# Attention probabilities turned by VectorE block transposes and DMA instead of TensorE, and the rotation split over VectorE, ScalarE and GpSimd

## The chip, the cores and the metric

The kernel runs on one core of one Trainium2 chip. The metric is the device time of one execution in microseconds (us). Engines: TensorE (PE, with its weight loads PEld), VectorE (DVE), ScalarE (ACT), GpSimd (POOL) and SyncE (SP), which here only issues DMAs. SPq and ACTq are the queues of SyncE and ScalarE. A line such as L305 is a line of the kernel before; lines of the changed kernel are named as such.

## What is computed

For each of 32 batches of 256 tokens with 128 features (cut from the reference):

```python
xn = layernorm(x)
# attention on xn
h = layernorm(xn) * ln_scale + ln_bias
c_q, c_kv = h @ w_down_q.T, h @ w_down_kv.T              # 64 latents each
q, k, v = (c @ w_up.T for ...)                           # 16 heads of 64
q, k = rope(q), rope(k)                                  # neighbouring columns e, o:
#   e*cos - o*sin, e*sin + o*cos
attn = softmax(q @ k.T / 8)                              # 256 x 256 per head
a = (attn @ v, heads side by side) @ w_out.T + xn
# feed-forward on xn, then 5 steps of an integrate-and-fire count
y = square(relu(xn @ W_fc.T)) @ W_proj.T
out = x + a + count_of_spikes(y) / 5
```

## The kernel before, in words

The unit of work is a pair of heads (128 rows: two heads of 64). A batch has 8 pairs, the program 256, numbered g. Each engine runs the same list of 256 steps plus some ahead of them. In step g it treats pair g + LEAD of each stage, so that pair g's stages lie in different steps: project 5 ahead, rotation 4, rounding 4 and 3, scores 2, transposes 1, weighing 0. `p` = g modulo 8 is the place of the step in its batch; work that occurs once a batch (normalising inputs, latents, feed-forward, output) hangs on certain p. Two batches (16 steps) are one loop body. Engines wait for one another by counting semaphores only, and each engine takes its list in order.

The stages of one pair:

- **project** (PE, L281, L282): q and k of the pair, 128 rows by 256 tokens each, into the one bank ps_qk; four fp32r matmuls (weights as high and low part).
- **rotate** (DVE, L604): two instructions multiply ps_qk by cosine and sine into cos_sin. **exchange** (SP, L242): two DMAs of 128 KB swap neighbouring rows of the sine part (odd rows to even, even to odd) into sin_sw. **add_rotated** (POOL, L745): qk = cosine part + sin_sw.
- **leading** (ACT, L498) and **rest** (POOL, L751): qk is split into two fp32r parts, qk_hi and qk_lo.
- **scores** (PE, L295): twelve fp32r matmuls (low x high, high x low, high x high, for two token halves t and two heads h); the heads use rows 0 to 63 and 64 to 127. Results stand in two banks, ps_s0 and ps_s1, one buffer each.
- **row_max** (DVE, L613): one per head; **exponentials** (ACT, L490): four, with sums into den; result prob.
- **transpose_probs** (PE, L305): eight 128x128 transposes into ps_t; **copy_transposed** (ACT, L503): two copies to prob_t.
- **weigh_latents** (PE, L319): four fp32 matmuls against the latents ckv into ps_u (the trace has two instructions for an fp32 matmul, so eight); **copy_u** (ACT, L510).

Once a batch: two halves of the feed-forward (PE L353, L363; ACT relu; POOL square), the count (DVE L666, L669, `integrate`, from a copy `drive` of y in SBUF), reciprocals of the sums (DVE L620 to L626, `invert_sums`), `normalise_u` (DVE L634, four), `attention_out` (PE L395, four steps with four instructions each), `add_spikes` (DVE L677), `finish` (DVE L684), input loads and output stores (SP L231, L235), `moments_of` (DVE L640, L646), `split_latents` (DVE L653, L658).

What sets the order is the list of each engine, written by hand in its `step` with the leads of one table:

```python
LEAD = {"project": 5, "add": 4, "lead": 4, "rest": 3, "scores": 2, "transpose": 1, "multiply": 0}
```

PE takes scores, transposes, projection, the once-a-batch work of this p, weighing. DVE takes the two row_max, then once-a-batch work, rotate, and more of it. ACT takes the exponentials, copy_transposed, leading, once-a-batch work, copy_u.

## Time and profile before

| | |
|---|---|
| median of 3 runs | 1274.29 us (1272.05 to 1274.43) |
| the profiled execution's own time | 1276.49 us |
| its span | 1274.4 us |
| busy: PE, DVE, ACT, POOL | 95%, 75%, 84%, 63% |
| mean granted clock of TensorE | 0.993 |
| one batch in mid-run (8 steps) | 38.97 us |
| moved by DMA | 80.03 MB, mean 63 GB/s |

The profiled execution is 2.1 us longer than its span (work around the first and the last instruction). Busy time is a union over instructions of an engine; a row's mean duration can be longer than its busy time divided by its count, since consecutive instructions overlap. GB/s and DMA shares are over the core's 16 DMA engines.

### The profile page before, as it was taken

The page shows a single profiled execution, that of the slowest core. Times are in us where ns is not written, and L with a number is a line of the kernel's source. Part 1 is how long each engine was busy: PE and PEld are TensorE (multiplying, and loading weights), DVE is VectorE, ACT ScalarE, POOL GpSimd, SP SyncE. Part 2 cuts the span into 40 slices and gives each one's busy share as a digit, 9 for nine tenths or more (in the row PEclk, how much of TensorE's full clock was granted, in tenths as well). Part 3 has the DMA queues.
Part 4 walks back from the last instruction along what each step waited for, and adds up shares of the span by engine and source line. Part 5 has one row for each costly group of instructions (what it writes and reads, how often), then busy time and mean ns, then how long its engine had stood idle before and what let it go on. Part 6 is the DMA issues. An engine that isn't in the chain of part 4 may idle for free.

```text
span 1274.4 us, 33640 instructions
## 1 busy us (share of the span) xinstructions
PE 1209.4 (95%) x9952; PEld 942.4 (74%) x9952; DVE 954.2 (75%) x1734; ACT 1074.4 (84%) x3425; POOL 806.8 (63%) x773
## 2 busy tenths in 40 slices
PE   4899999999999999999999999999999999999997
PEld 3767777777777777777777777777777777777775
DVE  3677777877778777778777778777778777778774
ACT  1788888888888888898888888888988888988884
POOL 2766676656666666666656667566666666666561
PEclk9899999999999999999999999999999999999999
DMA  4111111111111111111111111111111111111110
GB/s 132 68 55 59 60 67 68 58 60 57 65 67 63 62 61 55 66 66 59 66 53 63 66 61 64 62 58 63 62 62 67 58 58 66 60 65 66 59 63 21
DMA packets 60065, 80.03 MB, mean 63 GB/s; under 512 B 9664, under 2 KB 26304, under 8 KB 59840
## 3 DMA queue, kind: packets, MB, share of 16 engines
q1 hardware_dynamic: 59968, 79.11, 17.4%
q14 instruction: 81, 0.66, 0.2%
q8 instruction: 16, 0.26, 0.1%
HBM read 7.77 MB, written 4.19 MB: 9 GB/s over the span
## 4 chain that ended last, share of the span: by engine, by line
PE 59%; issue 18%; DVE 9%; POOL 8%; ACT 4%; DMA 1%; DVEq 0%; ACTq 0%; POOLq 0%; SPq 0%
PE ps_t L305 12%; PE ps_u L319 12%; PE ps_s L295 12%; PE ps_b L395 6%; PE ps_a L363 3%; PE ps_a L353 3%; POOL qk_lo L751 3%; PE ps_qk L281 3%; ACT prob L490 3%; DVE cos_sin L604 3%; PE ps_qk L282 3%; POOL qk L745 2%; PE ps_b L387 2%; DVE latent L653 2%; DVE neg_max L613 2%
## 5 line engine op out<-in xcount | busy, mean ns | idle before, releaser
L490 ACT ACTIVATE prob<-ps_s,neg_max 128x256 f32<-128x256 f32 x1024 | 473.0, 477 | 106.3 <-DVE neg_max L613 80.3
L751 POOL TENSOR_TENSOR qk_lo<-qk,qk_hi 128x512 fp32r<-128x512 f32 x256 | 327.4, 1279 | 328.8 <-ACT qk_hi L498 328.7
L613 DVE TENSOR_REDUCE neg_max<-ps_s 128x2 f32<-128x512 f32 x512 | 329.8, 686 | 247.3 <-PE ps_s L295 246.4
L745 POOL TENSOR_TENSOR qk<-cos_sin,sin_sw 128x512 f32<-128x512 f32 x256 | 334.9, 1308 | 83.7 <-DMA sin_sw<-cos_sin 81.3
L604 DVE TENSOR_TENSOR cos_sin<-ps_qk,rope_sb 128x512 f32<-128x512 f32 x512 | 328.8, 683 | 18.0 <-PE ps_qk L282 15.6
L305 PE MATMUL ps_t<-ident_sb,prob 128*128 128x128 f32 x2048 | 279.7, 280 | 0.4 <-ACT prob_t L503 0.4
L503 ACT COPY prob_t<-ps_t 128x512 f32<-128x512 f32 x512 | 278.1, 610 | 0.0
L319 PE MATMUL ps_u<-prob_t,ckv 128*64 128x256 f32 x2048 | 277.6, 392 | 0.0
L305 PEld LDWEIGHTS ps_t<-ident_sb,prob 128*128 128x128 f32 x2048 | 222.1, 141 | 31.2 <-issue 1.0
L490 ACT ACTIVATION_READ_ACCUMULATOR prob<-ps_s,neg_max 128x1 f32 x1024 | 211.1, 206 | 0.0
L319 PEld LDWEIGHTS ps_u<-prob_t,ckv 128*64 128x64 f32 x2048 | 124.2, 136 | 97.9 <-issue 48.2
L295 PE MATMUL ps_s<-qk_hi,qk_lo 64*128 64x256 f32 x1024 | 172.1, 331 | 13.7 <-ACT prob L490 13.3
L498 ACT CAST qk_hi<-qk 128x512 fp32r<-128x512 f32 x256 | 168.5, 658 | 16.3 <-POOL qk L745 15.4
L295 PEld LDWEIGHTS ps_s<-qk_hi,qk_lo 64*128 64x128 f32 x1024 | 98.0, 185 | 113.3 <-issue 112.4
L281 PE MATMUL ps_qk<-latent,wup_hi 128*128 128x256 f32 x512 | 155.8, 326 | 3.5 <-DVE cos_sin L604 3.5
L295 PE MATMUL ps_s<-qk_lo,qk_hi 64*128 64x256 f32 x1024 | 146.0, 279 | 0.0
L295 PE MATMUL ps_s<-qk_hi 64*128 64x256 f32 x1024 | 145.6, 278 | 0.0
L395 PE MATMUL ps_b<-u_n,wvo_sb 128*128 128x256 f32 x512 | 132.8, 383 | 0.8 <-DVE u_n L634 0.8
L282 PE MATMUL ps_qk<-latent,wup_lo 128*128 128x256 f32 x512 | 132.8, 281 | 0.0
L510 ACT COPY u_raw<-ps_u 128x256 f32<-128x256 f32 x256 | 104.4, 408 | 3.5 <-PE ps_u L319 3.5
L395 PEld LDWEIGHTS ps_b<-u_n,wvo_sb 128*128 128x128 f32 x512 | 95.7, 192 | 12.9 <-DVE u_n L634 1.0
L281 PEld LDWEIGHTS ps_qk<-latent,wup_hi 128*128 128x128 f32 x512 | 97.9, 191 | 4.4 <-DVE cos_sin L604 4.0
(64 smaller groups left out, 1440.9 us busy)
## 6 DMA issues: line engine op xcount, KB each, us to landing
sin_sw<-cos_sin SPq DMA_DIRECT2D x512, 128.0 KB, 2.1
x_sb<-in_x SPq DMA_DIRECT2D x32, 128.0 KB, 2.1
out<-out_sb SPq DMA_DIRECT2D x32, 128.0 KB, 2.0
wup_raw<-in_wup SPq DMA_DIRECT2D x2, 512.0 KB, 5.6
rope_sb<-in_rope SPq DMA_DIRECT2D x1, 512.0 KB, 6.6
wo_sb<-in_wo_t SPq DMA_DIRECT2D x1, 512.0 KB, 7.8
sel_raw<-in_sel SPq DMA_DIRECT2D x1, 512.0 KB, 8.6
wfc_sb<-in_wfc_t SPq DMA_DIRECT2D x1, 256.0 KB, 6.7
```

Of the source, the lines that this page charges most:

```text
L281: nc.tensor.matmul(bank, wup_hi[:, which, cols], rhs, start=True, stop=False)
L282: last = nc.tensor.matmul(bank, wup_lo[:, which, cols], rhs, start=False, stop=True)
L295: mm = nc.tensor.matmul(ps_s[h][:, t, :], q[rows, par, 0, t * P:(t + 1) * P], k[rows, par, 1, :], start=(n == 0), stop=(n == len(parts) - 1))
L305: last = nc.tensor.transpose(ps_t[h][:, kt, t * P:(t + 1) * P], prob[:, s % 2, h, t, kt * P:(kt + 1) * P], ident_sb[:, :])
L319: last = nc.tensor.matmul(ps_u[h * L:(h + 1) * L, 0:S], ckv[:, (s // PAIRS) % 2, kt, :], prob_t[:, s % 2, h, kt, :], start=(kt == 0), stop ...
L395: last = nc.tensor.matmul(ps_b[:, 0:S], wvo_sb[:, pair, :], u_n[:, pair, :], start=(pair == 0), stop=(pair == PAIRS - 1))
L490: last = nc.scalar.activation(prob[:, s % 2, h, t, :], ps_s[h][:, t, :], ACT.Exp, bias=neg_max[:, s % 2, h, t:t + 1], accum_out=den[:, bpa ...
L503: nc.scalar.copy(prob_t[:, s % 2, h, :, :], ps_t[h][:, :, :]).then_inc(pt_ready[h], 1)
L604: last = nc.vector.tensor_tensor(cos_sin[:, s % 2, :, which, :], ps_qk[:, which, :].unsqueeze(1).to_broadcast([P, 2, S]), rope_sb[:, which ...
L613: nc.vector.tensor_reduce(neg_max[:, s % 2, h, :], ps_s[h][:, :, :], AXIS_X, ALU.max, negate=True).then_inc(max_ready[h], 1)
L745: nc.gpsimd.tensor_tensor(qk[:, s % 2, :, :], cos_sin[:, s % 2, 0, :, :], sin_sw[:, s % 2, :, :], ALU.add).then_inc(rope_done, 1)
L751: nc.gpsimd.tensor_tensor(qk_lo[:, s % 2, :, :], qk[:, s % 2, :, :], qk_hi[:, s % 2, :, :].bitcast(F32), ALU.subtract).then_inc(lo_ready, 1)
```

## The change

- The scores are computed from qk in plain fp32: four matmuls (eight instructions) in place of twelve; qk_hi, qk_lo, the ACT cast and the POOL subtraction are gone. ps_s has two buffers (four banks).
- The rotation: DVE multiplies ps_qk by the cosine into qk (one instruction); ACT copies ps_qk as it is to `raw`; for two pairs at once ACT issues the two row-exchange DMAs (256 KB each) from its own queue, raw to `partner`; POOL multiplies partner by the sine and adds it to qk.
- The probabilities: ACT writes them so that the four 32-column blocks lie apart; DVE transposes all 32x32 blocks of a pair in one instruction (`turn`, 1024 elements a partition) into `turned`; for each GROUP of four pairs SP issues 16 DMAs (`move`, 128 KB each, from 32 partitions to 32 partitions) to `gathered`, which the weighing matmuls read. The eight PE transposes and the two ACT copies are gone.
- DVE reads y for the count from PSUM (the copy `drive` is gone); row_max is one instruction for both heads.
- Leads: project 11, rope 9, scores 7, turn 6. The once-a-batch work moves to other p.

The diff, cut to its core:

```diff
-LEAD = {"project": 5, "add": 4, "lead": 4, "rest": 3, "scores": 2, "transpose": 1, "multiply": 0}
-FIRST = -6
+LEAD = {"project": 11, "rope": 9, "scores": 7, "turn": 6, "multiply": 0}
+FIRST = -LEAD["project"]
+GROUP = 4
+Q = P // 32
...
+        turned = sb("turned", [P, 2, Q, GROUP, S])
+        gathered = sb("gathered", [P, 2, Q, GROUP, 2, 2, TT, 32])
+        raw = sb("raw", [P, 2, 2, 2, S])
+        partner = sb("partner", [P, 2, 2, 2, S])
+        qk = sb("qk", [P, 4, 2, S])
+        ps_s = pb("ps_s", [P, 2, 2, TT, S])
...
+            def move(g, s, half):
+                par = (s // GROUP) % 2
+                if half == 0:
+                    sp.wait_ge(turn_done, done(g))
+                    sp.sem_inc(sp_waited, 1)
+                    sp.wait_ge(u_ready, done(g - 2 * GROUP))
+                for rows in (2 * half, 2 * half + 1):
+                    for block_of in range(Q):
+                        sp.dma_start(gathered[32 * block_of:32 * block_of + 32, par, rows, :, :, :, :, :],
+                                     turned[32 * rows:32 * rows + 32, par, block_of, :, :]).then_inc(moved[par], 16)
...
+                if (s + turn) % GROUP == GROUP - 1 and not outside(g + turn, STEPS):
+                    move(g + turn, s + turn, 0)
+                if (s + turn) % GROUP == 0 and not outside(g + turn - 1, STEPS):
+                    move(g + turn - 1, s + turn - 1, 1)
...
             def scores(g, s):
-                pe.wait_ge(lo_ready, done(g))
-                for h in range(2):
-                    pe.wait_ge(exp_done[h], done(g - 1))
+                pe.wait_ge(rope_done, done(g))
+                pe.wait_ge(exp_done, done(g - 2))
...
+                        last = nc.tensor.matmul(ps_s[:, s % 2, h, t, :], qk[rows, s % 4, 0, t * P:(t + 1) * P],
+                                                qk[rows, s % 4, 1, :], start=True, stop=True)
...
             def weigh_latents(g, s, i):
-                for h in range(2):
-                    pe.wait_ge(pt_ready[h], done(g))
+                if s % GROUP == 0:
+                    pe.wait_ge(moved[(s // GROUP) % 2], (i * (BODY // GROUP // 2) + s // GROUP // 2 + 1) * 16 * Q * Q)
...
+            def copy_projected(g, s, i):
+                duo = s // 2
+                act.wait_ge(cos_ready, done(g))
+                if s % 2 == 0 and not outside(g - 4, STEPS):
+                    act.wait_ge(swapped[duo % 2], (i * (BODY // 4) + duo // 2) * 32)
+                nc.scalar.copy(raw[:, duo % 2, s % 2, :, :], ps_qk[:, :, :]).then_inc(raw_ready, 1)
+
+            def exchange(g, s):
+                duo = s // 2
+                act.wait_ge(rope_done, done(g - 4))
+                act.sem_inc(act_waited, 1)
+                act.wait_ge(raw_ready, done(g))
+                for odd in range(2):
+                    act.dma_start(partner[1 - odd::2, duo % 2, :, :, :], raw[odd::2, duo % 2, :, :, :])\
+                        .then_inc(swapped[duo % 2], 16)
...
             def rotate(g, s):
                 dve.wait_ge(up_ready, done(g))
+                dve.wait_ge(s_ready, done(g - 4))
+                nc.vector.tensor_tensor(qk[:, s % 4, :, :], ps_qk[:, :, :], cos_sb, ALU.mult).then_inc(cos_ready, 1)
...
+            def turn(g, s, i):
+                par = (s // GROUP) % 2
+                dve.wait_ge(exp_done, done(g))
+                if s % GROUP == 0 and not outside(g - 2 * GROUP, STEPS):
+                    dve.wait_ge(moved[par], (i * (BODY // GROUP // 2) + s // GROUP // 2) * 16 * Q * Q)
+                    dve.sem_inc(dve_waited, 1)
+                nc.vector.transpose(turned[:, par, :, s % GROUP, :],
+                                    prob[:, s % 2, :, :, :, :, :].rearrange("p j h k t c -> p j (h k t c)"))\
+                    .then_inc(turn_done, 1)
...
+                nc.gpsimd.tensor_tensor(other, other, sin_sb, ALU.mult).then_inc(sin_ready, 1)
+                pool.wait_ge(sin_ready, done(g))
+                pool.wait_ge(cos_ready, done(g))
+                nc.gpsimd.tensor_tensor(qk[:, s % 4, :, :], qk[:, s % 4, :, :], other, ALU.add).then_inc(rope_done, 1)
...
             def step(i, s):
                 g, b0, p = i * BODY + s, s // PAIRS, s % PAIRS
                 b = i * UNROLL + b0
+                if p == 5 and not outside(b - 1, B):
+                    add_spikes(b - 1, 1 - b0)
                 if not outside(g + LEAD["scores"], STEPS):
...
-                if p == 6 and not outside(b, B):
+                    row_max(g + LEAD["scores"], s + LEAD["scores"])
+                if p == 1 and not outside(b, B):
                     invert_sums(b, b0)
...
+                if p == 5 and not outside(b - 1, B):
+                    finish(b - 1, 1 - b0, i - 1 + b0)
+                if not outside(g + LEAD["turn"], STEPS):
+                    turn(g + LEAD["turn"], s + LEAD["turn"], i)
+                if not outside(g + LEAD["project"], STEPS):
+                    rotate(g + LEAD["project"], s + LEAD["project"])
```

The order on TensorE in the step with p = 4, before (a body's step: scores, transposes, projection, feed-forward, output, weighing):

```order
L295 MATMUL ps_s<-qk_hi,qk_lo 128x256 x2
L295 MATMUL ps_s<-qk_lo,qk_hi 128x256 x2
L295 MATMUL ps_s<-qk_hi 128x256 x2
L305 MATMUL ps_t<-ident_sb,prob 128x128 x8
L281 MATMUL ps_qk<-latent,wup_hi 128x256
L282 MATMUL ps_qk<-latent,wup_lo 128x256
L363 MATMUL ps_a<-hidden,wproj_sb 128x256 x2
L395 MATMUL ps_b<-u_n,wvo_sb 128x256 x2
L319 MATMUL ps_u<-prob_t,ckv 64x256 x4
```

and with the change (the step with p = 4 and the scores of the next; each lists a matmul once that the trace has twice):

```order
L292 MATMUL ps_s<-qk 128x256 x4
L363 ISA
L365 MATMUL ps_u<-ident_sb,rden_hl 128x128 x2
L325 MATMUL ps_a<-h_t,wdown_sb 128x256
L383 MATMUL ps_b<-u_n,wvo_sb 128x256 x2
L282 MATMUL ps_qk<-latent,wup_hi 128x256
L283 MATMUL ps_qk<-latent,wup_lo 128x256
L301 REGISTER_ALU
L308 MATMUL ps_u<-gathered,ckv 64x256 x4
L292 MATMUL ps_s<-qk 128x256 x4
```

The transposes are gone, the scores are four instead of twelve, and the weighing (which waits for `moved` in every fourth step, p = 0 and 4) stands right ahead of the next step's scores.

On DVE with the change, steps p = 1 and p = 2:

```order
L582 TENSOR_REDUCE neg_max<-ps_s 128x4
L598 RECIPROCAL rden<-den 128x32
L602 CAST rden_hl<-rden 128x2x16
L604 TENSOR_TENSOR rden_hl<-rden,rden_hl 128x2x16
L591 STREAM_TRANSPOSE turned<-prob 128x4x256
L577 TENSOR_TENSOR qk<-ps_qk,rope_sb 128x512
```

The last transpose of a group of four stands in the steps p = 1 and p = 5, behind row_max and, at p = 1, behind the three instructions of invert_sums.

On the queue of SP with the change, one batch:

```order
L230 DMA x_sb<-in_x 128x2x128
L241 REGISTER_ALU
L244 DMA gathered<-turned 32x1024 x16
L234 ISA
L234 DMA out<-out_sb 128x2x128
```

Of the 16 DMAs of a move (there are two moves a batch) all stand one behind another; the load of an input block stands behind a move on the same queue.

## Rows read from the trace of the kernel before

**Rows 1.** The page: busy time of each engine, and the chain that ended last.

```profile
PE 1209.4 (95%) x9952; PEld 942.4 (74%) x9952; DVE 954.2 (75%) x1734; ACT 1074.4 (84%) x3425; POOL 806.8 (63%) x773
...
PE 59%; issue 18%; DVE 9%; POOL 8%; ACT 4%; DMA 1%; DVEq 0%; ACTq 0%; POOLq 0%; SPq 0%
```

**Rows 2.** Busy time by window, three batches: window, length, engines, PEclk, DMA share, GB/s.

```profile
560.90:599.88 38.98, 37.28 (x312) 29.14 (x311) 29.23 (x55) 33.69 (x110) 25.45 (x25) 1.00 0.17 61
...
sum 116.90, PE 112.97 PEld 88.06 DVE 89.30 ACT 101.88 POOL 77.09; mean PE 37.66 PEld 29.35 DVE 29.77 ACT 33.96 POOL 25.70
```

**Rows 3.** Timeline of PE, one step: start, length (us), line, operation.

```profile
561.91 0.39 PE L295 MATMUL ps_s<-qk_hi,qk_lo 64*128 64x256 f32 x2
...
562.82 1.09 PE L305 MATMUL ps_t<-ident_sb,prob 128*128 128x128 f32 x8
563.66 0.37 PE L281 MATMUL ps_qk<-latent,wup_hi 128*128 128x256 f32 x1
...
564.22 1.02 PE L363 MATMUL ps_a<-hidden,wproj_sb 128*128 128x256 f32 x4
565.08 1.03 PE L395 MATMUL ps_b<-u_n,wvo_sb 128*128 128x256 f32 x4
566.04 1.08 PE L319 MATMUL ps_u<-prob_t,ckv 128*64 128x256 f32 x8
567.05 0.39 PE L295 MATMUL ps_s<-qk_hi,qk_lo 64*128 64x256 f32 x2
```

**Rows 4.** Groups of instructions by line, window 560.90:599.88 (one batch).

```profile
L604 DVE TENSOR_TENSOR cos_sin<-ps_qk,rope_sb 128x512 f32<-128x512 f32 x17 | 11.0, 683 | 0.4 <-PE ps_qk L282 0.4
L613 DVE TENSOR_REDUCE neg_max<-ps_s 128x2 f32<-128x512 f32 x16 | 10.3, 686 | 8.3 <-PE ps_s L295 8.3
...
L503 ACT COPY prob_t<-ps_t 128x512 f32<-128x512 f32 x17 | 9.3, 607 | 0.0
...
L498 ACT CAST qk_hi<-qk 128x512 fp32r<-128x512 f32 x8 | 5.3, 658 | 0.0
...
L510 ACT COPY u_raw<-ps_u 128x256 f32<-128x256 f32 x8 | 3.3, 408 | 0.0
...
L669 DVE SCALAR_TENSOR_TENSOR count<-drive,count 128x256 f32<-128x256 f32 x4 | 2.8, 708 | 0.0
```

**Rows 5.** Groups by form, whole span: DVE rows of other sizes and places.

```profile
L677 DVE SCALAR_TENSOR_TENSOR acc_t<-count,ps_b 128x256 f32<-128x256 f32 x32 | 13.5, 421 | 8.2 <-PE ps_b L395 7.3
...
L695 DVE TENSOR_TENSOR wup_lo<-wup_raw,wup_hi 128x2048 fp32r<-128x2048 f32 x1 | 2.3, 2293 | 0.0
...
L702 DVE CAST sel_sb<-sel_raw 128x1024 fp32r<-128x1024 f32 x1 | 0.7, 694 | 7.5 <-PE ps_b L416 7.5
```

**Rows 6.** DMA issues on SP, by line: duration min/median/max in ns.

```profile
L242 SPq DMA_DIRECT2D sin_sw<-cos_sin x512: 464/547/878, 28.3 to 1244.4; - x171
...
DMA to landing us min/median/max: 1.9/2.1/3.9
...
L231 SPq DMA_DIRECT2D x_sb<-in_x x32: 381/387/587, 0.7 to 1167.2; - x32
```

**Rows 7.** DMA in the first 20 us, in 40 slices of 0.5 us; issue to landing.

```profile
GB/s 0 0 0 44 217 63 112 91 246 246 311 246 246 213 246 213 137 178 235 410 344 373 356 373 389 430 397 418 410 393 328 8 0 0 0 0 0 0 0 0
...
wup_raw<-in_wup SPq DMA_DIRECT2D x2, 512.0 KB, 5.6
```

**Rows 8.** Timeline of PE: sixteen fp32 instructions (eight matmuls) of 64 rows.

```profile
23.99 1.04 PE L416 MATMUL ps_b<-wo_sb,wv_sb 64*64 64x128 f32 x16
```

**Rows 9.** The weighing matmuls: ns min/median/max, first and last start.

```profile
L319 PE MATMUL ps_u<-prob_t,ckv x2048: 379/379/507, 46.9 to 1260.9; 128*64 128x256 f32 x187
```

**Rows 10.** Busy time by window in the first 50 us; PEclk is the third number from the end.

```profile
31.20:34.10 2.90, 0.07 (x1) 0.03 (x1) 1.29 (x2) 1.67 (x4) 2.17 (x2) 0.91 0.24 90
34.10:39.60 5.50, 4.67 (x22) 3.42 (x23) 2.80 (x5) 3.42 (x12) 3.92 (x4) 0.50 0.13 48
...
43.90:47.00 3.10, 3.02 (x31) 2.77 (x32) 2.98 (x6) 2.56 (x9) 1.27 (x1) 1.00 0.15 48
```

More of the change, by code:

```diff
@@ L108, in build @@
         relu_sb = sb("relu_sb", [P, FC, S])
-        hidden = sb("hidden", [P, FC, S])
-        drive = sb("drive", [P, 2, S])
         count = sb("count", [P, 2, S])
@@ L162, in build @@
         acc_ready, fin_ready = sem("acc_ready"), sem("fin_ready")
-        t_ready = [sem(f"t_ready{h}") for h in range(2)]
-        pt_ready = [sem(f"pt_ready{h}") for h in range(2)]
+        turn_done = sem("turn_done")
+        moved = [sem(f"moved{i}") for i in range(2)]
         u_ready = sem("u_ready")
@@ L423, in extras @@
                 if not outside(n, B):
[L424 to L434 removed]
+                    if p == 0:
                         latents_by_token(n)
@@ L466, in step @@
                     scores(g + LEAD["scores"], s + LEAD["scores"])
-                if p == 7 and not outside(b, B):
+                if p == 4 and not outside(b, B):
                     transpose_rden(b)
-                if not outside(g + LEAD["transpose"], STEPS):
-                    for h in range(2):
-                        transpose_probs(g + LEAD["transpose"], s + LEAD["transpose"], h)
+                extras(b, b0, p)
                 if not outside(g + LEAD["project"], STEPS):
                     project(g + LEAD["project"], s + LEAD["project"], i)
-                extras(b, b0, p)
+                if p == 5 and not outside(b + 1, B):
+                    ffn_out(b + 1, 0)
                 if not outside(g, STEPS):
@@ L482, in _, with exponentials @@
         def _(act):
-            def exponentials(g, s, h, i):
-                act.wait_ge(max_ready[h], done(g))
-                act.wait_ge(t_ready[h], done(g - 2))
+            def exponentials(g, s, i):
+                act.wait_ge(max_ready, done(g))
+                act.wait_ge(turn_done, done(g - 2))
                 bpar, pair = (s // PAIRS) % 2, s % PAIRS
-                if pair == 0 and h == 0:
+                if pair == 0:
                     act.wait_ge(rden_ready, done(i * UNROLL + s // PAIRS - 2))
-                for t in range(TT):
-                    last = nc.scalar.activation(prob[:, s % 2, h, t, :], ps_s[h][:, t, :], ACT.Exp,
-                                                bias=neg_max[:, s % 2, h, t:t + 1],
-                                                accum_out=den[:, bpar, t, 2 * pair + h:2 * pair + h + 1])
-                last.then_inc(exp_done[h], 1)
@@ L709, in step @@
                 b = i * UNROLL + b0
+                if p == 5 and not outside(b - 1, B):
+                    add_spikes(b - 1, 1 - b0)
                 if not outside(g + LEAD["scores"], STEPS):
-                    for h in range(2):
-                        row_max(g + LEAD["scores"], s + LEAD["scores"], h)
-                if p == 6 and not outside(b, B):
+                    row_max(g + LEAD["scores"], s + LEAD["scores"])
+                if p == 1 and not outside(b, B):
                     invert_sums(b, b0)
-                if p == 7 and not outside(b - 1, B):
-                    add_spikes(b - 1, 1 - b0)
@@ L729, in step @@
                     split_latents(b + 2, b0)
-                if p == 7:
+                elif p >= 5:
                     if not outside(b, B):
-                        normalise_u(b, 0)
-                    if not outside(b - 1, B):
-                        finish(b - 1, 1 - b0, i - 1 + b0)
+                        normalise_u(b, p - 5)
+                    if p >= 6 and not outside(b + 1, B):
+                        for k in ((0, 1), (2, 3, 4))[p - 6]:
+                            integrate(b + 1, 1 - b0, k)
```

303 lines of the change are left out of this document (115 added, 188 removed).

## Prediction

> **What bounds the kernel now.** I read the page's busy shares and chain first, then the windows of three batches, then one step of PE's timeline, then the groups by line. PE is busy 95% and holds most of the chain [rows 1]. In mid-run a batch takes 38.97 us (116.90 / 3), of which PE is busy 37.66, ACT 33.96, DVE 29.77, POOL 25.70 [rows 2]. So 1.3 us a batch is idle time of PE, and the kernel is bound by PE's work. The timeline shows that work by its starts [rows 3]: scores 0.91 us (561.91 to 562.82), transposes 0.84, projection 0.56, half of the feed-forward 0.86, a quarter of the output 0.96, weighing 1.01. DMA is busy 17% [rows 2].
>
> I take all counts for one batch (8 pairs) and turn them into a time at the end.
>
> **PE.** The transposes go: 8 x 0.84 = 6.7 us less. The scores change from twelve fp32r instructions to eight fp32 ones. How long these take no row shows in this shape. The nearest is the weighing: eight fp32 instructions of the same 256 columns, two of them side by side in different parts of the array, 1.01 us [rows 3]. Sixteen instructions of 64 rows and 128 columns started within 1.04 us [rows 8], 0.065 each, while a full-size instruction of twice the columns takes 0.215 (0.86 / 4): pairs of 64 rows do run side by side in fp32. I take 1.01, thus +0.8 a batch. PE: 37.66 - 6.7 + 0.8 = **31.8 us**. Bounds: 0.91 as before, and 8 x 0.215 = 1.72 if the pairs run one after another (+6.5 in place of +0.8, a rival below).
>
> **DVE.** Rotation halves: 16 instructions of 10.35 us (11.0 x 16/17) become 8: -5.2 [rows 4]. The two row_max of 512 elements become one of 1024: 16 take 10.3, 0.644 each; from 512 to 2048 elements a two-input instruction grows from 683 to 2293 ns, 537 ns for 512 elements [rows 4, 5]; so one takes 0.644 + 0.537 = 1.18, eight 9.4: -0.9. The four `integrate` with two inputs in SBUF take 2.8; with y read from PSUM their form is that of L677, 421 ns: -1.1 [rows 4, 5]. Added: eight block transposes of 1024 elements. No transpose of DVE is in the trace. Below, a cast of 1024 elements takes 0.694 us; the instruction with one element a cycle would take about 1.18; 2.29 is what 2048 elements take [rows 5]. I take 1.18, since the plain copies near it that reach 0.69 are a mode of copies and casts: +9.4. DVE: 29.77 - 5.2 - 0.9 - 1.1 + 9.4 = **32.0 us**. It becomes as busy as PE.
>
> **ACT.** Gone: copies of transposes 9.3, cast 5.3, drive 0.4. Added: eight copies of ps_qk at about 0.58 (4.6) and eight DMA issues at 0.55 [rows 4, 6], 4.4, of which four times 0.4 lie beside copy_u (3.3 / 8). 33.96 - 15.0 + 4.6 + 2.8 = 26.4. It costs nothing: 5.4 us lie between it and PE. If an issue on ACT took three times as long, this cover would be gone.
>
> **POOL.** Two 512-element instructions a pair as before, 25.7: nothing. Its rotation runs two steps ahead of the scores (some 8 us), which hides the 2.1 us of the exchange [rows 6] and as much again.
>
> **The engines alone** thus allow 32.0 us a batch. Since the work hanging on p is uneven (PE heavy at p = 1 and 2, DVE at p = 4 to 0), I add 1.5, a little over PE's 1.3 now: 33.5.
>
> **The moves.** This is a new path, and I think that it ends last. A group of four pairs is moved after its last transpose (steps p = 1 and 5), and the weighing three steps later waits for it (p = 4 and 0). Behind that weighing in PE's list stand the next scores; behind these row_max, and behind it the last transpose of the next group. So once per group the loop is: move, weighing 1.01, scores 1.01 and 0.1 to their end, row_max 1.18, transpose 1.18, some 0.3 for four semaphores = move + 4.8. In one group `finish` (0.42) lies between, in the other `invert_sums` (1.0). Two groups make a batch: **batch = 2 x move + 9.6 + 1.4 = 2 x move + 11.0**. (The input load issued behind a move on SP reaches `moments_of` at p = 0 at about the same time, so it makes the same sum.)
>
> What a move takes: below, the issue decides. Sixteen issues at 0.39 to 0.55 us: the last begins after 5.8 to 8.2 and lands 2.1 later [rows 6], 7.9 to 10.3. Above, the transport decides: 16 x 128 KB are 2.10 MB, each DMA from 32 partitions into 32. While the two 64-partition loads wup_raw were under way the rate stood near 246 GB/s, later, with loads over 128 partitions, near 400 [rows 7]. At 0.246 MB/us a move is 8.5 us; the exchanges of ACT send 1.05 MB a group over the same engines, some 0.7 MB in that time, at 0.41 1.7 us; ahead of the first byte lie 1.8, and 0.1 for the semaphore. Sum **12.1 us**. If the exchange went at 0.246 too and wholly in the way (0.9 MB), 1.9 + 3.00 / 0.246 = 14.1. I take 12.1, nearer to the transport's rows than to the issue's, because the rate of 64 partitions is the nearest row to one of 32. That gives 35.2 us a batch, and PE and DVE idle over 3 us in it.
>
> The Trainium skill, "SBUF — State Buffer", section "Door 1: The DMA port swizzle", speaks against this change: 32 partitions reach only 8 of 16 ports, and 64 no more, with an asymptote of about 218 GB/s. By it an estimate of a move is 1.8 + 9.6 + 1.7 + 0.1 = 13.2 us, 37.4 a batch and 1252 us in all. The trace agrees in kind, with its 246 against 400 GB/s [rows 7].
>
> **Ends.** Before, the first weighing starts at 46.9, the last at 1260.9 [rows 9], and 13.5 us follow: 255 steps in 1214 where 31.9 batches of 38.97 would be 1243, so 29 are saved where stages are missing. With the change the fourth pair is transposed about when the first was weighed before, at 48; a move later, at 60, the first weighing starts. Of the 29 I keep 15, since a move does not shorten when stages are missing. The end stays at 14. Span = 60 - 15 + 14 + 31.9 x batch = 59 + 31.9 x batch.
>
> **Sum.** 59 + 31.9 x 35.2 = 1182 us. Against the profiled execution's own 1276.5 (its span plus 2.1) that is 1184; its median of three runs lies 2.2 lower, so **1182**. About 0.2% (2.5 us) is what a measurement of this kernel can tell from no change.
>
> **The rivals.**
>
> *A. The moves are hidden* and PE and DVE set the pace. For it: rows 6, by which a move may take 7.9 to 10.3 (a loop of 26.8 to 31.6, under 33.5). Against it: the 246 GB/s in rows 7. 59 + 31.9 x 33.5 = 1128 us; without any idle time 1080.
>
> *B. The moves are later than the cover: slower than before.* The place is the wait of the weighing at p = 0 and 4. It decides from 38.1 us a batch, that is from a move of 13.6 us. For it: with the exchanges in the way at the low rate a move is 14.1, a batch 39.2: 1309 us. Against it: packets of two queues need not add up, and the exchange spans all partitions.
>
> *C. The block transpose takes two cycles an element.* DVE 32.0 + 8 x 1.11 = 40.9, with 1.5 idle 42.4: 1412 us. For it only that no row shows the instruction. The Trainium skill, "Vector Engine (DVE) Microarchitecture Reference", says that the transposing array keeps up one element per cycle per lane; no row here can show it, and by it DVE stays at 32.0.
>
> *D. PE loses speed.* Either the fp32 score pairs run one after another (31.8 + 5.7 = 37.5, with 1.3 idle 38.8: 1297 us), so that the change would not do what it says for the scores; against it stand rows 8. Or the clock falls in the waits: after 2.9 us with 0.07 us of PE work it was 0.50 of full speed (1.2 GHz) for 5.5 us and more, and full again at 43.9 [rows 10]. In mid-run it stayed at 1.00 [rows 2]. Waits of 1.7 us (3.4 / 2) behind full work are shorter; were the clock low for a fifth of the batch, some 3 us would come on top: 1280 us.
>
> **How the numbers follow.** Forecast 53%, A 25%, B 11%, C 5%, D 6%. The forecast's own range, from a move of 11.2 to 13.3, is 33.5 to 37.6 a batch, 1128 to 1258. The range for 8 in 10 takes in most of A and the first half of B and D: 1100 to 1310. Faster: the forecast and A less 2 for a move near 13.6, 76%. Same: 3%. Slower: B, C, D with what is lost at the edge, 21%.
>
> **What would show it.** Right: DVE's transposes at 1.18 us; PE without transposes and near 31.8 us busy a batch; 90% busy PE and DVE; the weighing's idle time put down to the moves, 1 to 3 us twice a batch; a last landing some 12 us after the fourth transpose; the chain of waits with a share of DMA over 25% where it has 1% now [rows 1]. Wrong: no wait of PE for the moves (A); a wait over 4 us (B); transposes over 2 us (C); scores over 1.5 us or a granted clock under 0.95 (D); ACT busy over 90%, which I gave no case.

## The result: slower, 1368.8 us, and the profile after

The changed kernel takes 1368.81 us (median of 4 runs, 1363.53 to 1372.78), the kernel before 1274.2 on the same chip: ratio 1.0744 [1.0705, 1.0783]. The profiled execution took 1363.5 us, with a span of 1361.7 and a mean granted clock of 0.917. Forecast were 1182 and "faster"; it is rival B's side and beyond the range.

The page after: busy time, the clock in 40 slices, and the chain that ended last (against [rows 1]).

```profile
PE 1133.1 (83%) x6880; PEld 773.4 (57%) x6880; DVE 1048.2 (77%) x1478; ACT 823.7 (60%) x2881; POOL 793.1 (58%) x773
...
PEclk9888888998888999988998888998888998888998
...
issue 38%; PE 16%; POOL 16%; SPq 12%; DVE 9%; DMA 4%; ACT 4%; POOLq 1%; ACTq 0%; DVEq 0%
```

Busy time by window, three batches in mid-run (one of them and their sum; columns as in [rows 2]):

```profile
640.90:681.60 40.70, 34.75 (x216) 23.94 (x214) 32.41 (x46) 25.63 (x91) 25.55 (x26) 0.92 0.62 161
...
sum 122.00, PE 104.74 PEld 71.82 DVE 97.83 ACT 76.85 POOL 73.07; mean PE 34.91 PEld 23.94 DVE 32.61 ACT 25.62 POOL 24.36
```

A batch takes 40.7 us. ACT (25.6), POOL (24.4) and DVE (32.6) are within 1.4 us of their sums (26.4, 25.7, 32.0); only PE (34.9) lies well over its 31.8. And no engine is full. The new instructions, groups of the page:

```profile
L582 DVE TENSOR_REDUCE neg_max<-ps_s 128x4 f32<-128x1024 f32 x256 | 312.7, 1222 | 201.1 <-PE ps_s L292 197.8
...
L308 PE MATMUL ps_u<-gathered,ckv 128*64 128x256 f32 x2048 | 307.4, 425 | 35.2 <-DMA gathered<-turned 31.8
...
L591 DVE STREAM_TRANSPOSE turned<-prob 128x1024 f32<-128x1024 f32 x256 | 315.9, 1234 | 0.1
```

The block transpose takes 1.23 us (1.18 taken), so rival C falls. PE's waits (for what; us in total, times, longest), the longest and the one for the moves:

```profile
PE ps_a L331 <- DVE count L647: 72.4, 31, 2.5
...
PE ps_u L308 <- DMA gathered<-turned: 31.8, 47, 3.5
```

The wait for the moves is short: 0.5 us a weighing. That looks as if they hardly mattered. The timelines say otherwise (start, length in us). DVE's last transpose of a group, at p = 5:

```profile
747.09 1.23 DVE L591 STREAM_TRANSPOSE turned<-prob 128x1024 f32<-128x1024 f32 x1
```

PE three steps later, where the weighing at p = 0 needs it, with the scores of p = 1 behind it:

```profile
759.58 1.02 PE L331 MATMUL ps_a<-wkv_sb,h_t 128*128 128x64 f32 x4 [2.32 <-DVE count L647]
...
762.25 1.98 PE L308 MATMUL ps_u<-gathered,ckv 128*64 128x256 f32 x8 [0.26 <-DMA gathered<-turned]
764.16 2.08 PE L292 MATMUL ps_s<-qk 64*128 64x256 f32 x8
```

SP between the two, the sixteen issues of the move:

```profile
748.50 11.10 SPq L244 DMA_DIRECT2D gathered<-turned  x16
```

The transpose ends at 748.32; sixteen issues fill 11.1 us; 13.9 us after the transpose the weighing begins. Averaged over the moves in mid-run it is 13.9 us from the transpose to the weighing in both kinds of group, and 13.8 to the last landing. So the weighings at p = 0 and 4 start 0.13 us behind their last landing on average (0.23 at most): the moves' loop is closed, and the 2.3 us wait for the spike counts lies in its shadow. From a weighing to the end of the next group's last transpose pass 5.14 us at p = 4 and 7.86 us at p = 0. The sum 2 x 13.9 + 5.14 + 7.86 = 40.8 is the batch.

What the queues moved in that time (GB/s in slices of 0.4 us from 748.0; where ACT's exchange joins in, it goes to 389):

```profile
GB/s 0 0 0 0 205 215 215 195 164 277 195 174 225 195 236 174 184 266 297 389 205 205 318 246 328 266 215 164 256 205 195 246 129 179 214 224 12 0 0 0
```

The clock around p = 0 (windows; PEclk is the third number from the end):

```profile
716.20:718.50 2.30, 0.00 (x0) 0.00 (x0) 2.20 (x5) 1.41 (x6) 0.00 (x0) 1.00 0.94 257
718.50:721.00 2.50, 2.32 (x10) 2.02 (x10) 2.36 (x3) 1.02 (x5) 1.58 (x2) 0.55 0.84 192
721.00:723.00 2.00, 1.80 (x8) 0.77 (x8) 1.76 (x7) 1.56 (x6) 2.00 (x2) 0.50 0.20 59
723.00:725.00 2.00, 2.00 (x10) 1.19 (x8) 0.07 (x2) 0.37 (x1) 1.77 (x4) 0.50 0.24 96
725.00:726.00 1.00, 1.00 (x5) 0.83 (x4) 0.77 (x1) 0.00 (x0) 0.85 (x3) 0.71 0.84 332
726.00:731.00 5.00, 5.00 (x33) 3.68 (x32) 4.93 (x7) 3.28 (x11) 4.77 (x6) 1.00 0.05 12
```

Behind the 2.3 us without PE work the granted clock is 0.50 (1.2 GHz) for some 7 us, and the weighing and the scores at p = 0, both in the loop, take 1.98 and 2.08 us where they take 1.08 and 1.13 elsewhere (eight in a row, to the end of the last).

Theories for the experiments: **1**, SP's price for each of the sixteen issues makes the move, and the move makes the batch. **2**, the rival: transport makes the move. **3**, the low clock adds 2 us a batch. **4**, the exchange, issued by ACT at the same time, stretches the move.

### The profile page after: what moved, and what is told of

Its sections match the earlier page's. It is cut to its first block, busy times and chain, and to the rows that moved or that the text cites. A ratio compares the mean times of both kernels' runs of the same rounds, so it can differ in the third digit from the quotient of the medians.

```text
span 1361.7 us, 25592 instructions
## 1 busy us (share of the span) xinstructions
PE 1133.1 (83%) x6880; PEld 773.4 (57%) x6880; DVE 1048.2 (77%) x1478; ACT 823.7 (60%) x2881; POOL 793.1 (58%) x773
## 4 chain that ended last, share of the span: by engine, by line
issue 38%; PE 16%; POOL 16%; SPq 12%; DVE 9%; DMA 4%; ACT 4%; POOLq 1%; ACTq 0%; DVEq 0%
SPq L244 12%; POOL partner L725 7%; PE ps_s L292 5%; PE ps_u L308 5%; DMA gathered<-turned 4%; DVE turned L591 3%; POOL qk L728 3%; POOL relu_sb L757 2%; ACT prob L471 2%; PE ps_b L383 2%; DVE neg_max L582 1%; PE ps_a L344 1%; POOL rstd L740 1%; DVE qk L577 1%; POOL resid L750 1%
## 5 line engine op out<-in xcount | busy, mean ns | idle before, releaser
L725 POOL TENSOR_TENSOR partner<-partner,rope_sb 128x512 f32<-128x512 f32 x256 | 326.5, 1275 | 493.5 <-DMA partner<-raw 492.7
L582 DVE TENSOR_REDUCE neg_max<-ps_s 128x4 f32<-128x1024 f32 x256 | 312.7, 1222 | 201.1 <-PE ps_s L292 197.8
L728 POOL TENSOR_TENSOR qk<-qk,partner 128x512 f32<-128x512 f32 x256 | 327.7, 1280 | 20.1
L308 PE MATMUL ps_u<-gathered,ckv 128*64 128x256 f32 x2048 | 307.4, 425 | 35.2 <-DMA gathered<-turned 31.8
L292 PE MATMUL ps_s<-qk 64*128 64x256 f32 x2048 | 319.1, 434 | 7.0 <-POOL qk L728 7.0
L591 DVE STREAM_TRANSPOSE turned<-prob 128x1024 f32<-128x1024 f32 x256 | 315.9, 1234 | 0.1
L292 PEld LDWEIGHTS ps_s<-qk 64*128 64x128 f32 x2048 | 191.6, 202 | 131.3 <-issue 85.1
L577 DVE TENSOR_TENSOR qk<-ps_qk,rope_sb 128x512 f32<-128x512 f32 x256 | 171.3, 669 | 61.3 <-PE ps_qk L283 60.1
L308 PEld LDWEIGHTS ps_u<-gathered,ckv 128*64 128x64 f32 x2048 | 135.4, 147 | 127.4 <-issue 48.9
L483 ACT COPY raw<-ps_qk 128x512 f32<-128x512 f32 x256 | 152.6, 596 | 49.7 <-DVE qk L577 49.1
```

The source lines that it names most:

```text
L292: last = nc.tensor.matmul(ps_s[:, s % 2, h, t, :], qk[rows, s % 4, 0, t * P:(t + 1) * P], qk[rows, s % 4, 1, :], start=True, stop=True)
L308: last = nc.tensor.matmul(ps_u[h * L:(h + 1) * L, 0, :], ckv[:, (s // PAIRS) % 2, kt, :], gathered[:, (s // GROUP) % 2, :, s % GROUP, h, k ...
L577: nc.vector.tensor_tensor(qk[:, s % 4, :, :], ps_qk[:, :, :], cos_sb, ALU.mult).then_inc(cos_ready, 1)
L582: nc.vector.tensor_reduce(neg_max[:, s % 2, :, :], ps_s[:, s % 2, :, :, :], AXIS_X, ALU.max, negate=True).then_inc(max_ready, 1)
L591: nc.vector.transpose(turned[:, par, :, s % GROUP, :], prob[:, s % 2, :, :, :, :, :].rearrange("p j h k t c -> p j (h k t c)"))\
L725: nc.gpsimd.tensor_tensor(other, other, sin_sb, ALU.mult).then_inc(sin_ready, 1)
```

## The experiments

The kernel before took 1274 to 1275 us beside all of them, and every ratio is to it. The diffs are cut to their core. "Move" is the mean time from the last transpose of a group to the last landing, over 44 moves in mid-run; "batch" the mean of 22.

### What a move is made of

**Half the bytes**, `e1_half_bytes`.

```diff
-gathered[..., par, rows, :, ...], turned[..., par, block_of, :, :]
+gathered[..., par, rows, 0:2, ...], turned[..., par, block_of, 0:2, :]
```

> Left out: only two of the four pairs of a group are moved (1 KB runs doubled to 2 KB of the 4 KB per partition), the other two are read from a constant fill; still sixteen DMAs a move, each of 64 KB in place of 128 KB. Theory 1 (the fixed price of an issue on SP, some 0.6 us a DMA whatever its size, decides): issues keep their spacing of 0.63 us, a move stays at 12 to 14 us, total 1320 to 1365. Theory 2 (transport decides: 32 partitions take the bytes at about 0.2 MB/us and SP is held back by its full queue): issue spacing falls to about 0.3 to 0.4, a move to 7 to 8 us, the loop to under 28 us a batch, so that PE and DVE set the pace: some 33 to 36 us a batch, 1110 to 1210 in all.

Measured: 1270.56 us, ratio 0.995 [0.9927, 0.9973]. Neither range was hit. By line, all issues of the move:

```profile
L244 SPq DMA_DIRECT2D gathered<-turned x1024: 507/591/1742, 55.2 to 1255.1; - x171
```

The issues take what they took with 128 KB (507/592/1922), spaced 0.66 in place of 0.70 us: theory 1 holds for the issues. But the last landing comes 1.8 us sooner (12.05), and at 12.05 the moves stop binding: the weighings start 0.6 and 1.4 us after the last landing. The batch is 37.7, and that is what the engines need, not the 33.5 I had given them.

**Twice the issues for the same bytes**, `e2_issues_x2`.

```diff
+for pairs in (slice(0, 2), slice(2, 4)):
-    sp.dma_start(gathered[..., rows, :, ...], turned[..., block_of, :, :])
+    sp.dma_start(gathered[..., rows, pairs, ...], turned[..., block_of, pairs, :])
```

> The same bytes in 32 DMAs of 64 KB in place of 16 of 128 KB. Theory 1 (price per issue): a move takes 32 x 0.6 + 2.5 = some 22 us, a batch 2 x 22 + 11 = 55, in all 59 + 31.9 x 55 = some 1810 us. Theory 2 (transport): spacing 0.31 to 0.4, a move 14 to 15 us, in all 1360 to 1430 us.

Measured: 1936.86 us, ratio 1.5204 [1.5148, 1.526]; move 22.0, batch 58.7. SP's timeline for one move, and PE's wait:

```profile
613.36 20.34 SPq L245 DMA_DIRECT2D gathered<-turned  x32
```

```profile
PE ps_u L310 <- DMA gathered<-turned: 553.4, 63, 12.8
```

Spacing 0.64 us with half the bytes in each: theory 2 falls as the cause of the spacing. The 1810 of theory 1 was short because the rest of the loop took 7.85 and 6.68 us in place of 11.0 together, at a mean clock of 0.798.

**No exchange**, `e3_no_exchange`.

```diff
-act.dma_start(partner[1 - odd::2, ...], raw[odd::2, ...])
-nc.gpsimd.tensor_tensor(other, other, sin_sb, ALU.mult)
+nc.gpsimd.tensor_tensor(other, raw[:, duo % 2, s % 2, :, :], sin_sb, ALU.mult)
```

> Left out: the exchange of neighbouring rows; the rotation takes its sine part from the unswapped copy, so 67 MB and 256 issues of ACT are gone. Theory 1 in its form with contention (ACT's two DMAs in the middle of a move stretch SP's issues there from 0.6 to 1.1 us and the landing from 2.2 to 4.7): spacing 0.6 throughout, a move 16 x 0.6 + 2.3 = 11.9 us, 2 us less than now, a batch 4 us shorter, in all 1230 to 1250 us. If the moves were limited by their own issue alone, with no such contention: within 10 us of 1365.

Measured: 1287.46 us, ratio 1.0106 [1.0069, 1.0144]. Spacing 0.630, move 12.0, as theory 4 had it; so the exchange beside it adds 1.8 us to a move. The total that I expected from it (1230 to 1250) was missed, since a batch is 38.5, and the weighings begin 0.7 to 1.2 us after the landing: the engines' floor again. This run has almost exactly the move that I forecast (12.1), and it is no 1182.

**The exchange back on SP**, `e12_exchange_sp` (one part of the change undone).

```diff
 move(g + turn, s + turn, 0)
+exchange(g + LEAD["project"], s + LEAD["project"])   # was in ACT's step
 move(g + turn - 1, s + turn - 1, 1)
```

> The exchange is begun from SP's queue again, between the two halves of a move where both fall into one step. Theory 4 (ACT's queue is the right place, since SP's issues decide): the move gets two issues more, 2 x 0.63 us, and loses the stretching by ACT's queue, some 1 us; exchanges behind a move come up to 5 us late and hold back the scores: 1365 to 1480. Rival (the changed queue itself costs, through ACT's time or two queues at once): under 1350.

Measured: 1394.83 us, ratio 1.0934 [1.0899, 1.097]. Moves of 14.1 and 15.0, each weighing 0.13 to 0.14 us behind the landing. Beginning the exchange from ACT's queue is thus worth some 26 us here; it isn't what made the change slow.

**Four of sixteen issues on ACT**, `e5_split`.

```diff
-sp.dma_start(gathered[...], turned[...])    # rows == 3
+act.dma_start(gathered[...], turned[...])   # rows == 3, at the end of ACT's step
```

> Four of the sixteen DMAs of a move are issued by ACT at the end of its step instead of by SP; the rest is the changed kernel. Theory 1 (SP's issues, 0.63 to 0.70 us each, set the move and the move sets the loop): a move falls from 13.9 to 12 x 0.68 + 2.4 + 0.3 = some 11 us, the loop to 33 us a batch, under what the engines themselves need, some 37.7 as in the run with half the bytes: in all 1265 to 1285. Rival (transport or contention in the queues, which two issuers do not relieve): over 1340.

Measured: 1349.0 us, ratio 1.059 [1.0572, 1.0608]. SP's last issue now begins 7.6 us after the transpose in place of 10.6, but the last landing is at 10.6 in one group and 12.2 in the other (where the exchange is issued before SP's last), 3.1 and 4.6 us behind it, against the 2.4 of `e3_no_exchange`. I read this as transport setting the end of a move once the issues are relieved. It falls out of the loop (0.8 and 4.7 us of room), and the batch still is 40.5. I put this down to ACT's 2.5 us of issues (four of 0.63), which come in front of its other work. PE's waits:

```profile
PE ps_a L331 <- DVE count L658: 67.2, 31, 2.5
PE ps_a L320 <- ACT z_sb L520: 66.3, 31, 3.3
```

The second was 33.3 in the changed kernel. My expectation missed this price.

### The waits and the clock

**PE's wait for the spike counts**, taken away in two ways. `e4_late_lif_wait` writes the latents by token into the weighing's bank:

```diff
-    pe.wait_ge(lif, ...); matmul(ps_a[:, t * L:(t + 1) * L], h_t[...], wkv_sb)
+    pe.wait_ge(u_evac, ...); matmul(ps_u[:, 1, t * L:(t + 1) * L], h_t[...], wkv_sb)
```

> The latent product for the tokens of the next batch goes to the free half of the weighing's bank, and PE's wait for the last spike count is put one step later, where it has long come. Theory 3 (the 2.3 us wait in front of that product and the half clock after it cost some 2 us a batch): the granted clock rises from 0.917 to over 0.97, a batch falls to some 39 us, in all 1295 to 1310. Rival (the moves' loop sets the pace, and the idle time and the low clock only move to the weighing's wait at p = 0): idle time of the weighing put down to the moves rises by some 2 us a batch, the clock stays near 0.92, in all 1350 to 1370.

Measured: 1396.99 us, ratio 1.0966 [1.0905, 1.1027]. Worse than either theory, since the weighing at p = 0 now waits for ACT's copy of that bank (78 us in all), 1.0 us beyond its landing. `e6_counts_early` only reorders DVE:

```diff
+if p == 7: integrate(k = 2, 3, 4)   # ahead of row_max
-if p == 7: integrate(k = 2, 3, 4)   # at the end of the step
```

> The last three spike counts stand ahead of row_max at p = 7 on DVE instead of at the end of that step, so that PE's 2.3 us wait for them at p = 0 goes; the moves stay. Theory 1 (the loop of the moves decides, PE's idle time and low clock only pass to the weighing's wait): 1345 to 1370. Theory 3 (the wait and the half clock behind it cost 2 us a batch by themselves): 1290 to 1310.

Measured: 1372.97 us, ratio 1.0782 [1.0762, 1.0801]. The wait is gone and the time is not: PE waits 1.9 us for `u_n` instead and 51.8 us in all for the moves (31.8 before). The loop decides. The mean clock stays low too, at 0.912. `e7_order_only` takes two more waits out (inputs' transposes behind the projection and `copy_u` ahead of `copy_inputs` at p = 3).

```diff
+if p == 3: transpose_inputs(b + 2, b0)   # PE, behind project
+if p == 3: copy_u(g, s, i)               # ACT, ahead of copy_inputs
```

> Three waits between engines are taken out by order alone: the counts early on DVE at p = 7, the inputs' transposes behind the projection at p = 3, and ACT's copy of u ahead of the inputs' copies at p = 3. The moves stay as they are. Theory 1: the loop of the moves still decides, 2 x 13.9 + 11.0 = 38.9 us a batch and what the low clock adds: 1300 to 1365. If the engines' own waits were the limit: some 4 us a batch less, 1240 or under.

Measured: 1366.4 us, ratio 1.0721 [1.0704, 1.0739]; batch 41.0. Nothing again. `e8_split_order` puts it together with the split of the issues (both diffs above).

> Both: ACT issues four of the sixteen DMAs, and the three waits are taken out by order. Theory: two limits stand near each other, the moves (now some 33 us a batch) and the engines' waits (37.7, with these three gone some 34 to 36): 1150 to 1220 us, under the kernel before. If the engines' floor were not made of these waits: 1265 to 1285, as the split alone.

Measured: 1322.63 us, ratio 1.0358 [1.0337, 1.0378]. The same order is worth 26 us now that the moves bind in one of the two groups at most (3.97 us of room in the other), but it stays far above the 1150 to 1220 that I expected. PE now waits 42.8 us in all for ACT's copy `raw` (4.6 in the changed kernel); that ACT's issues cause this, I only argue.

**The clock by itself**, `e9_fillers`.

```diff
 scores(...)                        # p == 0
+6 x matmul(ps_u[:, 1, :], wdown_sb, h_t)
 ...
+3 x matmul(ps_u[:, 1, :], wdown_sb, h_t)
 weigh_latents(g, s, i)
```

> The changed kernel, with nine full-size matmuls of 0.21 us each into an unused half bank put where PE waits at p = 0 (six after the scores, three ahead of the weighing); their results are never read. They add 2 us of PE work a batch and remove nothing. Theory 3 (after the wait PE works at half clock, and that makes the weighing at p = 0 take 1.97 and the scores behind it 2.01 us in place of 1.08 and 1.13, 1.8 us of the moves' loop a batch): granted clock over 0.96, a batch some 2 us shorter, in all 1300 to 1320. Rival (the clock does not matter to the loop): 1365 to 1440.

Measured: 1353.16 us, ratio 1.0611 [1.0583, 1.0639], clock 0.991. The way from the weighing at p = 0 to the end of the next last transpose falls from 7.86 to 5.29 us, 2.6 us a batch. Of this 1.8 us lie on PE: row_max begins 3.96 us behind the start of the weighing in the changed kernel and 2.20 here. So the clock's price is 1.8 us a batch, near theory 3's 2. The fillers gave back 1.8 us by holding that weighing 1.8 us beyond its landing, and the total fell by only 16 us.

The other 0.8 us lie behind row_max, on DVE. They are mostly the small cast of `invert_sums`. The changed kernel, POOL and DVE, and then the same cast in `e9_fillers`:

```profile
767.41 1.27 POOL L725 TENSOR_TENSOR partner<-partner,rope_sb 128x512 f32<-128x512 f32 x1 [0.79 <-DMA partner<-raw]
767.80 0.92 DVE L602 CAST rden_hl<-rden 128x32 fp32r<-128x32 f32 x1
```

```profile
760.14 0.18 DVE L611 CAST rden_hl<-rden 128x32 fp32r<-128x32 f32 x1
```

In the changed kernel 20 of the 32 casts start while POOL multiplies `partner`, take 0.92 to 1.32 us, and each ends 0.04 us behind that multiplication; the other 12 take 0.18. The mean in mid-run is 0.8 us, against 0.19 in `e9_fillers`. So the fillers took this price away only by moving the cast in time.

### The loop opened, and the floor behind it

**One step more of lead**, `e10_lead12`, and with the three changes of order, `e11_lead12_order`.

```diff
-LEAD = {"project": 11, "rope": 9, "scores": 7, "turn": 6, "multiply": 0}
+LEAD = {"project": 12, "rope": 10, "scores": 8, "turn": 7, "multiply": 0}
+if p == 4: split_latents(b + 2, b0)   # ahead of turn, was behind rotate
```

> Projection, rotation, scores and transpose run one step further ahead (12, 10, 8 and 7 pairs in place of 11, 9, 7 and 6), and the split of the latents stands ahead of the transpose at p = 4; the moves themselves are unchanged, but four steps lie between the last transpose of a group and its weighing in place of three. Theory 1: the moves fall out of the limit, and the engines' floor of some 37.7 to 38.5 us a batch remains, as in the runs with half the bytes and without the exchange: 1270 to 1300. Rival (contention or the length of the moves acts in some other way than through this wait): over 1340.

> The same lead, and the three changes of order (counts early at p = 7, inputs' transposes behind the projection at p = 3, u copied ahead of the inputs). Theory: without the moves as a limit the waits between engines are the limit, and taking three of them out gives 1 to 2 us a batch: 1200 to 1250 us, under the kernel before. If order moved nothing here either: 1270 to 1300.

Measured: 1292.71 us, ratio 1.0159 [1.0108, 1.021], and 1281.41 us, ratio 1.0046 [1.0033, 1.006]. Moves are as long as ever (13.6 to 13.8), the weighings 3 to 6 us behind them, and 76 us are gone: the moves' loop was the main loss. The clock rose with it from 0.917 to 0.973, so that its price is a part of the 76. Order adds 11, less than expected. Batches of 38.4 and 38.0 are the floor of the first runs.

What the floor is, the windows of one batch of `e1_half_bytes`, about one window a step from p = 0, show (PE is the first number behind the length, DVE the third):

```profile
677.10:682.90 5.80, 3.47 (x30) 2.36 (x28) 5.56 (x8) 3.43 (x15) 3.59 (x3) 1.00 0.56 160
682.90:687.50 4.60, 4.50 (x30) 3.21 (x28) 4.29 (x12) 2.99 (x14) 3.33 (x7) 1.00 0.29 114
687.50:692.30 4.80, 4.55 (x30) 3.22 (x28) 4.24 (x5) 4.49 (x17) 4.61 (x4) 1.00 0.28 67
692.30:697.10 4.80, 4.10 (x32) 2.90 (x30) 3.07 (x3) 3.76 (x14) 1.45 (x2) 1.00 0.61 170
697.10:702.30 5.20, 4.23 (x30) 2.98 (x28) 3.26 (x4) 4.39 (x17) 3.80 (x4) 1.00 0.30 84
702.30:707.80 5.50, 4.37 (x30) 2.80 (x28) 5.41 (x10) 2.91 (x11) 4.28 (x4) 1.00 0.24 95
707.80:711.70 3.90, 3.90 (x30) 2.75 (x28) 2.91 (x4) 2.03 (x9) 3.73 (x4) 1.00 0.41 101
711.70:714.60 2.90, 2.90 (x24) 1.90 (x22) 2.87 (x6) 1.34 (x6) 0.00 (x0) 1.00 0.57 164
sum 37.50, PE 32.03 PEld 22.11 DVE 31.59 ACT 25.34 POOL 24.79; mean PE 4.00 PEld 2.76 DVE 3.95 ACT 3.17 POOL 3.10
```

PE needs 32.03 and DVE 31.59 (forecast 31.8 and 32.0), but in different steps: DVE fills the first and sixth, PE the second, third, seventh and eighth. Adding the busier of the two over the eight windows gives 35.2. A projection needs ACT's copy of the last one, which needs DVE's rotation, which needs the projection: the two engines are tied once a step, and their surpluses don't average out. The test puts the same DVE work into other steps.

```diff
+if p in (2, 3):    # e15; (6, 7) in e16
+    nc.vector.tensor_tensor(unread[:, p % 2, :, :], cos_sb, cos_sb, ALU.mult)
```

> The version with the lead of twelve and the three changes of order, with one more DVE multiplication of 512 elements (0.65 us, its result never read) at p = 2 and one at p = 3, where PE has more to do than DVE. Theory of the floor (projection, rotation, copy and the next projection tie PE and DVE together once a step, so that a batch is the sum of each step's longer engine and not the longer of the two sums): these 1.3 us a batch lie in DVE's idle time: 1281 to 1295. Rival (DVE's sum over the batch decides): 1281 + 31.9 x 1.3 = some 1322.

> The same two multiplications at p = 6 and p = 7, where DVE has more to do than PE. Theory of the floor by steps: each of them costs its full time, 31.9 x 1.3 = 42 us, in all 1312 to 1328. Rival (sums over the batch, with room of 5 us on DVE): as at p = 2 and 3.

Measured: 1280.81 us, ratio 1.0061 [1.0032, 1.0091], and 1366.56 us, ratio 1.0724 [1.0695, 1.0752], to be set against the 1281.41 us of `e11_lead12_order`. At p = 2 and 3 the two multiplications cost nothing, at p = 6 and 7 they cost 85 us, where I expected 31 to 47. They were not the 0.65 us each that I had taken: those at p = 2 and 6 take 0.68 and 0.67 us, those at p = 3 and 7 1.35 and 1.62 on average in mid-run. All 62 that take longer than 0.8 us start beside an instruction of POOL and end 0.55 us behind it, much as the cast above. So 2.0 us a batch went in for nothing in one run, and 2.3 us (73 in all) cost 85 in the other. PE's longest group of waits in the second:

```profile
PE ps_b L376 <- DVE u_n L614: 93.7, 62, 4.1
```

It was 16.2 us in `e11_lead12_order`, and the clock falls from 0.980 to 0.949: PE is busy 1119.2 us in place of 1077.1 with the same 6880 instructions. The theory by steps holds in kind, since by sums over the batch the two runs would have come out alike; how much of the 85 us is the clock stays open.

**Two waits of that floor.** ACT begins the exchange ahead of `copy_u` (`e13_exchange_first`), PE projects behind the weighing at p = 4 (`e17_late_project`), or both (`e14_exchange_first_late_project`), all on `e11_lead12_order`.

```diff
-project(...)               # PE, ahead of weigh_latents
+if p != 4: project(...)
 weigh_latents(g, s, i)
+if p == 4: project(...)
 ...
+exchange(...)              # ACT, ahead of copy_u
 copy_u(g, s, i)
-exchange(...)
```

> The version with the lead of twelve and the three changes of order, and in it ACT begins the exchange right behind its copy of the projection instead of behind its copy of u, which waits for the weighing. Theory: of the 56 us that the scores waited for POOL's rotation there (it waits for the exchange, 5.3 us on its way beside a move), most go: 1235 to 1270 us, under the kernel before. If the exchange's wait hides other waits behind it: within 10 us of 1281.

> As the one before, and the projection at p = 4 stands behind the weighing on PE, since it waited 1.5 us a batch for the split of the latents there: another 20 to 40 us less than the run before, if the waits add up. If the steps' longer engine decides and not these waits: within 10 us of it.

> The projection at p = 4 behind the weighing, in the version with the lead of twelve and the three changes of order, and the exchange left behind the copy of u, where the changed kernel has it. In the pair of runs 13 and 14 the exchange begun earlier came with 9 us more than the 1281 without it, the late projection with 26 us less. If the two add up: 1255, within 5 us. If the projection's gain hung on the earlier exchange: 1264 to 1281.

Measured: 1290.41 us, ratio 1.012 [1.0093, 1.0147]; 1264.0 us, ratio 0.9917 [0.9885, 0.9949]; 1262.23 us, ratio 0.9907 [0.9887, 0.9926]. The early exchange gained nothing: the scores' wait for POOL stayed at 51.5 us (56.1 without it), and for the scores that wait longest the exchange began no sooner ahead of the weighing that ends the step before them (5.6 us in both). The late projection takes most of the wait for the split (46.8 us, then 8.3) away and 19 to 26 us with it. The last is the lowest time found, level with the one before it, and 0.9% below the kernel before; its page:

```profile
PE 1086.1 (86%) x6880; PEld 730.7 (58%) x6880; DVE 1024.2 (81%) x1478; ACT 817.4 (65%) x2881; POOL 791.6 (63%) x773
```

## Why the prediction was wrong

**Right:** the engines' busy times (PE 32.03 at full clock against 31.8; DVE, ACT and POOL within 1.4 us); fp32 score pairs that run side by side (1.13 us, the weighing 1.08); the transpose; the loop itself (5.14 us at p = 4 where I had 4.8 + 0.42); and the ends, 1361.7 - 31.9 x 40.8 = 60, against 59. A batch came out at 40.8 in place of 35.2 by two large terms and a small one:

- **The move, 12.1 taken, 13.9 measured: 2 x 1.8 x 31.9 = 115 us.** The step that failed is "below, the issue decides ... above, the transport decides". I priced an issue at 0.39 to 0.55 us from [rows 6] and left 0.55 as an upper end; the new issues take 0.59, start every 0.63 us, and every 0.70 with the exchange beside them: 10.5 us from the first to the last. The 0.547 of [rows 6] hid this: it is the median of two kinds, since in the kernel before the first issue of each pair took 0.47 us and the second 0.60. Without the exchange the last landing comes after 12.0 us (`e3_no_exchange`: 0.1 + 15 x 0.63 + 2.4), where my sum without it was 10.3 (1.8 + 8.5); the exchange adds 1.8, where I had 1.7. So the miss is the issues' share. And I took issue and transport for two bounds of which one holds. Here they are nearly equal, and beside the exchange they add at the end: the last landing is 3.1 us behind the start of the last issue, not 2.1. The 8.5 us for transport was no bad figure: in `e5_split`, with the issues relieved, a move without an exchange in its way lands 10.6 us after the transpose, 8.2 after its first landing. The rule that 32 partitions reach an asymptote of about 218 GB/s (the Trainium skill, "SBUF — State Buffer", "Door 1: The DMA port swizzle") agrees with the 195 to 215 GB/s of the first slices of the move, but halving the bytes showed that this rate came from the spacing of the issues: 128 KB every 0.63 us are 208 GB/s.
- **The clock: 1.8 x 31.9 = 57 us.** Rival D had the mechanism, and 3 us a batch for a clock that is low a fifth of the time, but I gave it 6%. I argued that waits of 1.7 us behind full work are shorter than the 2.9 us in [rows 10]. Here the clock fell at a wait that no term of mine had, 2.3 us for the spike counts, which the change puts there, and it struck the two PE pieces that lie in the loop. The length of that wait alone does not decide, though: `e1_half_bytes` has the same 2.3 us in each batch (its window 677.10:682.90 above, with the clock at 1.00) and a mean clock of 0.978, and in `e6_counts_early` no wait of PE in mid-run is over 1.9 us and the clock still falls once a batch. What decides stays open.
- **DVE's part of the loop: 0.2 x 31.9 = 6 us.** It took 0.3 us more at p = 0 than my sum, by the cast that ends with POOL's multiplication, and 0.1 less at p = 4.

1182 + 115 + 57 + 6 = 1360, and the span is 1361.7. But a right move would not have saved the forecast: **"the engines alone ... I add 1.5"** failed as well. Their floor is 37.5 to 38.5 us a batch, shown by the runs in which no move binds, so rival A was worth 59 + 31.9 x 37.7 = 1262 us and not 1128. With it, and a move of 12.1, the forecast would have read 1262. I had seen that the work hangs unevenly on p, and priced it at a little over PE's idle time in the kernel before, in which only PE was near full.

The sign that I had named for the forecast, over 25% of DMA in the chain of waits, was no good either: DMA has 4%, SP's queue 12% and "issue" 38%. Nor was rival B's, a wait over 4 us: the longest for a move is 3.5 and the mean 0.5. Only D's did appear, a clock under 0.95.

Rival B was the one on the right side, with 11%. It too had the loop, and its 14.1 us for a move by the wrong road (the exchange at the low rate); the runs show the issues.

Not tried: the shorter rotation, the fp32 scores and the counts from PSUM by themselves. Also open is how the rest of 37.5 over 35.2 divides.

## What to carry to other kernels

When work moves from an engine to DMA, count the instructions that start it, take their price from rows of the same kind of transfer (here SBUF to SBUF with few partitions, 0.59 us against the 0.39 of an input load), look whether a median mixes two kinds, and put the whole chain of starts and the last landing into the dependence loop. A short wait in front of the consumer does not say that a loop is open: compare when the data lands with when the consumer starts. Where two engines hand work to each other every step, add up the longer of them step by step; the sums of busy time gave a bound that none of the orders tried here came near. And price a small DVE instruction where it stands: beside POOL's work it can take as long as that.

## What the runs showed of the hardware

- On SP, starting an SBUF-to-SBUF DMA over 32 partitions took 0.591 us at the median with 64 KB and 0.592 with 128 KB; the input's load from DRAM over 128 partitions takes 0.39 [rows 6]. Beside an exchange the 12th to 14th of a move took 0.85, 1.19 and 0.78 us at the median (0.59 in `e3_no_exchange`), single ones up to 1.9, and the mean spacing rose from 0.630 to 0.70 us.
- An exchange of 2 x 256 KB landed 2.9 us after its first issue by itself, and 5.6 beside a move.
- In the changed kernel the granted clock halved once a batch, at the wait of 2.3 us, mostly for some 7 us. In `e1_half_bytes` 24 of 26 such waits in mid-run left it at 1.00, and in `e6_counts_early` it halved once a batch with no wait of PE over 1.9 us in mid-run.
- A DVE cast of 128x32 elements took 0.18 us by itself; started while POOL multiplied 128x512 elements in SBUF, it ended 0.04 us behind POOL (20 of 20 in the changed kernel). A DVE multiplication of 128x512 with both inputs in SBUF took 0.67 to 0.68 us, and in the same position ended 0.55 us behind POOL (62 of 62 in the last two DVE runs).
- Nine matmuls more a batch whose results nobody reads made the kernel faster (1353 against 1369 us).
